# Adapter columns of each sample gathered on their own, in place of all adapters' columns, and weights of the next block loaded after three of four splits

## The reference, cut to what matters

```python
def _lora_linear(x, W, A, B, adapter_indices):
    base = jnp.einsum('bsd,df->bsf', x, W)
    Ai = A[adapter_indices]
    Bi = B[adapter_indices]
    lora = jnp.einsum('bsr,brf->bsf', jnp.einsum('bsd,bdr->bsr', x, Ai), Bi)
    return base + lora
gate = _lora_linear(x, Wg, Ag, Bg, adapter_indices)
up = _lora_linear(x, Wu, Au, Bu, adapter_indices)
h = jax.nn.silu(gate) * up
return _lora_linear(h, Wd, Ad, Bd, adapter_indices)
```

## Time and profile before

| | us |
|---|---|
| median of 3 runs | 1263.4 |
| lowest and highest | 1262.7, 1264.01 |
| profiled execution | 1261.51 |
| its span | 1259.5 |
| PE busy | 1248.5 |
| POOL busy | 665.2 |

### The profile page before, as it was taken

The page is one execution under the profiler, slowest core; times in us unless marked ns, Lnnn a source line. Parts: engine busy times, 40 slices in busy tenths (PEclk is TensorE's granted clock), DMA queues, the critical chain, the costliest instruction groups (busy, mean ns, idle before and its releaser), DMA issues.

```text
span 1259.5 us, 17908 instructions
## 1 busy us (share of the span) xinstructions
PE 1248.5 (99%) x6204; PEld 1042.1 (83%) x6204; DVE 976.8 (78%) x1554; ACT 559.4 (44%) x993; POOL 665.2 (53%) x549
## 2 busy tenths in 40 slices
PE   8999999999999999999999999999999999999998
PEld 7788888888888888888888888888888888888887
DVE  7987777886788777788779768777878877777775
ACT  4644445444344454454444444544443434434332
POOL 4476555555635556545554556565555444444553
PEclk9999999999999999999999999999999999999999
DMA  6856345555965345446687544544487732233423
GB/s 197 296 179 219 122 119 166 159 146 167 374 208 192 105 124 149 127 133 176 213 322 215 161 126 142 153 124 130 143 287 279 231 86 91 76 117 101 114 90 116
DMA packets 141096, 210.11 MB, mean 167 GB/s; under 512 B 43472, under 2 KB 87760, under 8 KB 141008
## 3 DMA queue, kind: packets, MB, share of 16 engines
q1 hardware_dynamic: 118128, 137.03, 35.2%
q0 software_dynamic: 22016, 70.80, 16.8%
q10 hardware_dynamic: 864, 1.15, 0.3%
HBM read 164.89 MB, written 44.04 MB: 166 GB/s over the span
## 4 chain that ended last, share of the span: by engine, by line
PE 91%; DVE 4%; DMA 2%; issue 1%; ACT 1%; another core or an unknown queue 0%; SPq 0%; DVEq 0%; ACTq 0%
PE px L1549 28%; PE pd L1549 27%; PE py L1549 14%; PE pz L1549 7%; PE pz L1566 3%; PE pv L1595 2%; PE pv L1593 2%; PE pd L1827 2%; PE py L1566 2%; PE px L1566 1%; DVE wg_lo L1215 1%; DMA w_raw<-w_gu 1%; PE pd L1576 1%; PE pd L1670 0%; PE pd L1798 0%
## 5 line engine op out<-in xcount | busy, mean ns | idle before, releaser
L687 POOL TENSOR_TENSOR h_lo<-g,h_hi 128x512 fp32r<-128x512 f32 x127 | 184.2, 1450 | 334.9 <-ACT h_hi L809 334.1
L656 POOL DMA_INDIRECT b_got<-b_table,idx_b x192 | 197.5, 1029 | 58.8 <-issue 49.3
L1549 PE MATMUL px<-xo_hi,wg_hi 128*128 128x512 f32 x540 | 216.8, 402 | 1.9 <-DVE xo_lo L1227 0.6
L1347 DVE TENSOR_TENSOR acc<-pd,acc 128x512 f32<-128x512 f32 x252 | 167.9, 685 | 63.2 <-PE pd L1549 57.6
L1215 DVE TENSOR_TENSOR wg_lo<-w_raw,wg_hi 128x512 fp32r<-128x512 f32 (+1 forms) x268 | 192.1, 720 | 31.5 <-ACT wg_hi L809 18.8
L1549 PE MATMUL px<-xo_hi,wg_lo 128*128 128x512 f32 x540 | 211.8, 392 | 0.0
L1549 PE MATMUL px<-xo_lo,wg_hi 128*128 128x512 f32 x540 | 210.3, 389 | 0.0
L809 ACT ACTIVATE wg_hi<-w_raw 128x512 fp32r<-128x512 f32 (+1 forms) x272 | 153.0, 570 | 115.1 <-PE py L1566 72.3
L1549 PE MATMUL pd<-wd_hi,h_hi 128*128 128x512 f32 x512 | 202.8, 396 | 0.0
L1549 PE MATMUL pd<-wd_lo,h_hi 128*128 128x512 f32 x512 | 201.0, 393 | 0.0
L1549 PE MATMUL pd<-wd_hi,h_lo 128*128 128x512 f32 x512 | 199.8, 390 | 0.0
(11 more groups left out here) (292 smaller groups left out, 2401.2 us busy)
## 6 DMA issues: line engine op xcount, KB each, us to landing
w_raw<-w_gu SPq DMA_DIRECT2D x68, 512.0 KB
wd_raw<-w_dn SPq DMA_DIRECT2D x64, 256.0 KB
xo_hi<-xops SPq DMA_DIRECT2D x21, 512.0 KB, 5.9
xo_lo<-xops SPq DMA_DIRECT2D x21, 512.0 KB, 6.9
acc<-x SPq DMA_DIRECT2D x8, 1024.0 KB, 8.3
ad_raw<-ad_table SPq DMA_DIRECT2D x16, 512.0 KB
xops<-st_hi SPq DMA_DIRECT2D x24, 256.0 KB, 2.8
xops<-st_lo SPq DMA_DIRECT2D x24, 256.0 KB, 2.9
```

The source lines that it names most:

```text
L656: gp.indirect_dma_start(out=dst, out_offset=None, in_=rows_of, in_offset=bass.IndirectOffsetOnAxis(ap=rows.bitcast(U32), axis=0)).then_inc ...
L687: return gp.tensor_tensor(dst, src_raw, src_hi, ALU.subtract)
L1347: ins = dve.tensor_tensor(dst, pd[j][:, :], dst, ALU.add)
L1549: ins = pe.matmul(psum, w_parts[wi], x_parts[xi], start=(start and i == 0), stop=(stop and i == 2), skip_group_check=more)
```

## The change

The columns of all eight adapters are no longer multiplied in quarters 2 to 4 (the first quarter is as it was, with its own code). Instead POOL gathers, for each of the quarter's 16 samples, the 32 input columns of its own adapter (`gather_own`: 16 gathers of 128 rows of 512 bytes) into `st_lo` in blocks 13 to 15. ACT and DVE split them in four groups, and PE multiplies them with the tokens in two pieces of 24 matmuls with 256 columns (`own_products`): one between the two last down phases, one after them. The 0/1 matrix no longer depends on the quarter: ACT makes it once, in block 14 of the first quarter, from masks that DVE makes in block 13. Small tables move into other buffers to make room. SP, POOL, ACT and DVE have a new order at the change of quarter, and `next_weights` waits for three groups and the sums, and skips the unit that has no weights any more. The diff, cut to its core; helpers and SP:

```diff
+        def own(cp):
+            return flat(st_lo[:, :, :]).rearrange("p (s c e) -> p s c e", s=QS, c=KC)[:, :, 2 * cp:2 * cp + 2, :]
...
+        def own_homes(g):
+            if g == 3:
+                return u[:, 0, 1, 0:2 * WH], u[:, 1, 1, 0:2 * WH]
+            return flat(wg_hi[:, 2 * g:2 * g + 2, :]), flat(wg_lo[:, 2 * g:2 * g + 2, :])
+        def summed_units(n):
+            return n - n // UNITS
...
             def next_weights(n):
-                for g in range(4):
+                if (n + 1) % UNITS == 0:
+                    return
+                for g in range(3):
                     sp.wait_ge(w_done[g], n + 2)
-                load_weights(n + 2)
+                sp.wait_ge(t_done, 4 * summed_units(n + 1))
+                load_weights(n + 2 if (n + 2) % UNITS else n + 3)
...
+                k_done = blocks_done(q, b)
+                if b == -1 and q:
+                    for g in range(2):
+                        store_ad(q, g)
+                if b >= 0 and b % AD_BLOCKS == 0 and n > 1:
+                    load_ad(q, b // AD_BLOCKS)
...
-                    for done, k in ((p1_mm, A11), (p5_mm, S1), (p6_mm, S2), (p2_mm, A12), (p7_mm, S3), (p3_mm, S4),
-                                    (p4_mm, A22)):
-                        sp.wait_ge(done, n)
+                    for done, k in ((p1_mm, A11), (p5_mm, S1), (p2_mm, A12), (p4_mm, A22), (p6_mm, S2), (p7_mm, S3),
+                                    (p3_mm, S4)):
+                        sp.wait_ge(done, k_done)
                         for g, xo in enumerate((xo_hi, xo_lo)):
                             sp.dma_start(raw(xo[:, k, :]), xops[g, k]).then_inc(xop_in[k], 16)
-                    next_weights(n)
...
+            def gather_own(q, samples):
+                for s in samples:
+                    home = flat(st_lo[:, :, :])[:, s * P:(s + 1) * P]
+                    gather_rows(home, a_in_rows, idx_own[:, (q - 1) * QS + s:(q - 1) * QS + s + 1], own_got[s // (2 * TP)])
...
+                if to_own and b % 2:
+                    if b == BLOCKS - 3:
+                        for half in range(2):
+                            gp.wait_ge(xops_out[half], TP * (q + 1) * 64)
+                    gather_own(q + 1, {-3: range(8, 11), -1: range(4, 7)}[b - BLOCKS])
...
                     gp.wait_ge(*piece_out(max(0, m - 1)))
-                    gp.wait_ge(p3_mm, n)
-                    gather_b(to_q, m, 0)
-                if b == BLOCKS - 2 and q + 1 < QUARTERS:
-                    for g in range(2, AD_GROUPS):
-                        gather_ad(q + 1, g)
+                    gp.wait_ge(p3_mm, k)
+                    if to_own and b == BLOCKS - 1:
+                        if q == 0:
+                            gp.wait_ge(bd_out, 2 * 16)
+                        else:
+                            gp.wait_ge(bdown_mm, q * QP)
+                        gp.wait_ge(xops_out[0], TP * (q + 1) * 64)
+                        gather_bd(q, 0)
+                    else:
+                        gather_b(to_q, m, 0)
...
-                    gp.wait_ge(p4_mm, n)
+                    gp.wait_ge(p4_mm, k)
+                    if to_own and b == BLOCKS - 1:
+                        gather_b(to_q, m, 0)
                     gather_b(to_q, m, 1)
...
-                    for half in range(2):
...
+                if to_own and b == BLOCKS - 1:
+                    for g in range(4):
+                        gp.wait_ge(w_done[g], n + 2)
                     for g in range(2):
                         gather_ad(q + 1, g)
-                if b == BLOCKS - 1 and q + 1 < QUARTERS:
```

ACT and DVE:

```diff
             def weights_high(n, g):
+                if n % UNITS == 0:
+                    if g < 3:
+                        act.wait_ge(own_got[g // 2], n // UNITS * 2 * TP * 16)
+                    else:
+                        act.wait_ge(own_diff, n // UNITS)
+                    src, hi_part, _ = own_group(g)
+                    copy(hi_part, src).then_inc(w_hi_done[g], 1)
+                    return
...
                 if b == -1:
...
                     v_lower(q - 1, 0)
                     v_high(q - 1, 0)
+                    ua_high(q, 0)
+                    weights_high(n + 1, 0)
+                    weights_high(n + 1, 1)
+                    weights_high(n + 1, 3)
                     v_lower(q - 1, 1)
...
+                    ua_high(q, 1)
+                    weights_high(n + 1, 2)
+                    v_high(q - 1, 1)
+                    continue
...
-                if b == -1:
-                    ua_high(q, 0, 0)
-                    ua_high(q, 1, 1)
-                    ua_high(q, 0, 1)
...
-                    v_high(q - 1, 1)
-                    weights_high(n + 1, 3)
-                    continue
+                if (q, b) == (0, BLOCKS - 2):
+                    act.wait_ge(sel_mm, 2)
+                    act.wait_ge(slots_done, 1)
+                    for m in range(2):
+                        for s in range(HS + 2):
+                            lo, hi = s * SAMPLE_ROWS, min((s + 1) * SAMPLE_ROWS, SEL_COLS)
+                            at = 2 * (s % HS) + m
+                            ins = act.activation(sel_own[:, m, :, lo:hi], pattern_kept[:, :, 0:hi - lo], ACT.Copy,
+                                                 scale=slot_mask[:, at:at + 1])
...
+                if to_own:
+                    for g in range(4):
+                        weights_high(n + 1, g)
...
+                dve.tensor_scalar(idx_own[:, :], adf[:, QS:SAMPLES], float(P), p_f[:, 7:8], ALU.mult, ALU.add)
...
+            def own_difference(q):
+                dve.wait_ge(own_got[1], q * 2 * TP * 16)
+                first, last_two = (own(cp)[:, 2 * TP:QS, :, :] for cp in range(2))
+                dve.tensor_tensor(last_two, last_two, first, ALU.subtract).then_inc(own_diff, 1)
...
                 if b == -1:
-                    v_low(q - 1, 0)
-                    c11(n)
-                    u3(n)
-                    ua_low(q, 0, 0)
-                    c12(n)
-                    ua_low(q, 1, 1)
-                    ua_low(q, 0, 1)
-                    sums(n + 1)
-                    weights_low(n + 1, 0)
-                    ua_low(q, 1, 0)
+                    ua_low(q, 1)
+                    finish(q - 1, 0, (0,))
+                    weights_low(n + 1, 2)
                     select(q, 0)
-                    weights_low(n + 1, 1)
-                    weights_low(n + 1, 2)
-                    finish(q - 1, 0)
-                    weights_low(n + 1, 3)
-                    selectors(q, 1)
+                    finish(q - 1, 0, (1, 2, 3))
                     continue
                 if b == 0:
                     if q:
                         v_low(q - 1, 1)
-                    c11(n)
-                    u3(n)
+                        sums(n + 1)
+                    c11(k)
+                    if q:
+                        weights_low(n + 1, 0)
+                    u3(k)
                     if not q:
                         sums(n + 1)
                     select(q, 1)
                     if not q:
...
-                        sums(n + 1, low=True)
...
+                if (q, b) == (0, BLOCKS - 3):
+                    dve.wait_ge(layer_mm, QP)
+                    dve.tensor_copy(pattern_kept, pattern)
+                    for at in range(2 * HS):
+                        ins = dve.tensor_scalar(slot_mask[:, at:at + 1], p_f[:, 0:1], float(at), None, ALU.is_equal)
+                    ins.then_inc(slots_done, 1)
+                if not last and not late and not to_own:
                     sums(n + 1)
                 if parts_at(q, b) is not None:
...
-                c11(n)
+                if to_own:
+                    own_difference(q + 1)
...
+                if to_own:
+                    sums(n + 2)
...
+                    if to_own and not phase_at[2]:
+                        v_low(q, 0)
+                        ua_low(q + 1, 0)
+                        weights_low(n + 1, 2)
+                        weights_low(n + 1, 3)
+                        for g in (0, 1, 3):
+                            weights_low(n + 2, g)
```

PE (removed: the branches `if adapters:` of the seven products):

```diff
             def select(q, t):
-                pe.wait_ge(ua_done, 4 * q + max(ua_order(q, t, m) for m in range(2)))
-                pe.wait_ge(sel_done, 2 * q + t + 1)
+                pe.wait_ge(ua_done, ua_made(q, t))
...
                         for part, ua in enumerate((h_hi, h_lo)):
-                            ins = pe.matmul(select_bank(q, t, m, c), sel[:, part, c * P:(c + 1) * P], ua[:, t, m, tokens],
-                                            start=(part == 0), stop=(part == 1))
+                            if q:
+                                first = c * P % SEL_REPEAT
+                                rows, ua_m = sel_own[:, m, part, first:first + P], ua[:, t, 0, tokens]
+                            else:
+                                rows, ua_m = sel[:, part, c * P:(c + 1) * P], ua[:, t, m, tokens]
```

(30 more changed lines are left out.)

313 lines of the change are left out of this document (159 added, 154 removed).

## The result

The changed kernel is slower: 1275.8 us median of four runs (1274.6 to 1278.1) against 1263.7 (1262.7 to 1264.65), a ratio of 1.0104 with a 95% interval of 1.0091 to 1.0117. The forecast was 1257.0, with a range up to 1262.8. The span went from 1259.5 to 1274.4 us.

What follows compares the result with a forecast made beforehand. PE bounds the kernel, busy 1248.5 of 1259.5 us. Per change 4.09 - 1.54 = 2.55 us; three give 7.65, less 1.2 paid once, 6.45 us: median 1263.4 becomes 1257.0, 8-in-10 range 1251.3 to 1262.8.

Steps and rivals of the forecast that it cites:

- The matmuls: PE at each change of quarter: 48 products at 0.1175 us, 5.64 us, replace 9.53 us of matmuls, gaining 3.89 us.
- the third rival: Weight loads not hidden in the 48 products: 188 ns each, 9.0 us per change, 1262.5 us; chance 0.03.
- Own columns in time: At `own_products`, from the end of block 15's first down phase: no PE wait, up to 0.3 us at the bound.
- Paid once: First quarter: selector copies in block 14 cost 1.0 us, index instructions 0.6, early loads return 0.4; sum 1.2 us.
- The new wait: Block 0 after each change: PE waits 1.54 us for masks that stand on DVE behind the load of block 1's weights.
- No gather landed later than 7.0 us, those in full stretches included: Argument against the rival of late own columns: every gather in the trace landed within 7.0 us.
- own columns that come late: Rival: PE waits at the first `own_products` for a split behind a late gather; slower, 1273.3 us; chance 0.05.
- Block 1: Block 1 of the new quarters: its wait for block 2's sums is covered, load out near 981.3, c11 due at 987.
- no queue at SP: Condition, with a quick gather, of the rival that block 1's weights land by 970.2: no new wait; chance 0.24.
- they land late: Rival: block 1's weights land at 974.2, wait 4.0 us, gain 0.05 us per change, 1264.5 us; chance 0.14.
- no new wait: Rival: block 1's weights land by 970.2, gain 4.09 us at each of three changes, 1252.3 us; chance 0.24.

Runs made afterwards that it cites:

- experiment 8: Kernel before, weights loaded after three groups and the sums instead of four groups: 1260.8 us, ratio 0.9990; experiment 3 with four groups again: 1256.5 us, ratio 0.9947.
- experiment 5: Kernel before, with only the changed kernel's order: next block's sums and splits ahead of c11 in blocks 0 and 1 of quarters 2 to 4; 1287.0 us, ratio 1.0190.
- experiment 7: Changed kernel without the loads of the tokens' low parts at each change of quarter (3.5 of 7 MB): 1261.8 us, ratio 0.9981.
- experiment 6: Changed kernel with 22 unused matmuls added on PE where it waits for the masks, block 0 of quarters 2 to 4: 1270.8 us, ratio 1.0066.
- experiment 1: Changed kernel with SP issuing the load of block 1's weights ahead of the two down-adapter stores: 1267.2 us, ratio 1.0043.
- experiment 2: Changed kernel with block 1's sums and splits back behind the gate in block 0 of quarters 2 to 4: 1266.0 us, ratio 1.0035.
- experiment 3: Changed kernel with the next block's sums and splits back behind the gate in blocks 0 and 1 of quarters 2 to 4: 1251.6 us, ratio 0.9912.
- experiment 4: Experiment 3 plus experiment 1's SP edit, block 1's weights loaded ahead of the stores: 1252.1 us, ratio 0.9913.

## Where the prediction held and where it failed

- **The matmuls** held: 48 products at 0.12 us, 5.74 us in place of 5.64. The weight loads were hidden and the third rival was wrong. The Trainium skill (TensorE: Matmul & The Clock Gate, The mechanism) says in its list of what overlaps that a load does so only in another row group, though the paragraph above that list also lets a load go ahead into a background weight buffer. The pitch of 0.12 us with a new weight for each product, where a load's row is 190 ns long, decides against the list here and fits the paragraph.
- **Own columns in time** held: PE waited neither at the first `own_products` nor at the second, in any of the three changes, and the 48 own gathers landed after 2.4 to 6.2 us.
- **Paid once**, forecast 1.2 us: the copies cost 0.87 us in block 14 (forecast 1.0), block 1 with the index instructions 0.16 (forecast 0.6), 0.5 us came back in blocks 2 to 12, as with the early loads in experiment 8, and the first mark was 0.43 us ahead already. The sum was 0.09. Of this the first mark is luck: between executions of code that is the same up to there it moves by over 1 us (1.4 us later in experiment 5 than in the kernel before).
- **The new wait** is the step that failed. Its mechanism was named rightly, place and releaser too, and the term of the sum was mis-sized: 1.54 us, where 6.19, 5.71 and 5.37 were measured. The working, against the start of block 0 at the third change (964.74 forecast, 974.86 measured): the second gather started 4.4 us ahead of it (3.2 forecast), but landed after 8.28 us and not some 5.2; so the weights' load was issued 4.4 us behind it (2.8 forecast) and let DVE start 10.8 us behind it (7.0 forecast). The two landings were the median of all such gathers and a load of block 14, from stretches with less under way (the share of the DMA engines is 0.67 from 919 to 927 us in the kernel before, and 0.98 from 970.5 to 978.8 us, while this gather is under way); for the traffic now beside them the prediction charged the time of one transfer, 1.3 us, and never added up the bytes. "No gather landed later than 7.0 us, those in full stretches included" was a misreading: the trace has a landing for 16 of the 296 gathers of that line, all of down adapters, the last one issued at 930.0 us, ahead of the token loads (938.05 us). The low parts of the tokens alone cost the gather 2.7 us (experiment 7). That "the token loads cannot hold the gather up for long" was argued, for the own gathers, from the Trainium skill (DMA: Bandwidth & Descriptors, Queues, rings and completion order): the own gathers bear it out, but engines may take turns between rings, and a gather of the down adapters still takes 8.28 us behind the token loads. The bound for "late" had the same fault, 4.0 us. A slower kernel had a chance of 0.07, and its case was another one, own columns that come late.
- **The clock** is missing from every case of the prediction. It was halved behind each of the three waits of over 5 us, which cost some 5 to 6.5 us in all (experiment 6): the waits cost their own 17.3 us and about a third more.
- **Block 1** failed, with a wait put at nothing: "c11 there is due only at 987". The change puts the sums of block 2 ahead of c11 in block 1 as well (`late`). c11 itself was in time; u3, which stands behind the sums, c11 and a split, was not, and PE waits 0.7 us for it. Block 1 gave away 1.93, 0.79 and 1.91 us; 0.9 us of each is this wait (experiment 6), and the other 1.0 us at the first and third change is the low clock of the first wait. In experiments 1 and 2, where block 0 has next to no wait, PE waits for c11 too, by up to 2.56 and 3.24 us.
- **The reason for the wait** was seen from one side. The prediction named the new place of the sums, but laid the length of the wait on POOL and SP, since the load stands behind the stores, and had no wait at all with "no queue at SP". Against block 0 the load is not later than it was: it went out at 974.67 in the kernel before (SP's timeline, below), 6.0 us behind the start of block 0, and now 4.4 us behind it. In the kernel before nothing in PE's path stood behind it: the first sum starts 11.9 us behind the start of block 0, with no wait (DVE's timeline), and in the changed kernel the load lets DVE start 11.6, 11.1 and 10.8 us behind it. It would have been in time for the old place.

```profile
974.67 0.33 SPq L483 DMA_DIRECT2D w_raw<-w_gu  x1
980.55 0.42 DVE L1202 TENSOR_TENSOR w_raw<-w_raw 128x256 f32<-128x256 f32 x1
```

  Experiments 3, 4 and 5 show it from both sides: with the old place of the sums the new SP order costs nothing, with the new place even the old SP order costs 24 us. Experiment 1 shows what the prediction had right: a load that goes out 0.3 us ahead of block 0 takes block 0's wait away too, but it is then some 4 us earlier than the changed kernel's and 6 us earlier than in the kernel before.

The rival "they land late" came closest, with no change as its end; the forecast of 1252.3 for "no new wait" is within 1 us of what the change gives without that order (1251.6), partly by luck: it gains less per change than was forecast (3.1 and not 4.09 us) and paid nothing once only, since the profiled execution was 0.9 us ahead at the end of the first quarter.

## What to carry to other kernels

An instruction that waits for a transfer makes everything behind it on its engine wait for that transfer: before moving it forward, compare when the transfer lands now, in the rows, with when the next thing behind it is due; here it was enough that the load had never been early enough for the new place, whatever its queue. Where a change packs transfers together, add up the bytes of the stretch and take landings from a stretch that is as full. And price a wait of some microseconds on TensorE at its length plus what a low clock behind it costs, here 1.4 to 2.5 us for a wait of 5.4 to 6.2 us.

## What was not expected of the hardware

- Behind 5.4 to 6.2 us without a matmul TensorE's granted clock was 0.50 and stayed there for 3.3 to 5.8 us of work; the products of 512 columns went from 0.23 to 0.43 us of pitch. With shorter waits it went either way: 2.56 us (experiment 1) and 2.33 us (experiment 2) were followed by a clock of 0.50, 2.25 us (experiment 1) and 2.57 us (experiment 7) were not. Executions of experiment 1 differ by 7 to 9 us, at mean clocks of 0.998 and 0.991 to 0.994.
- 66 matmuls of no use made the kernel about 5 us faster.
- A gather of 512 KB landed after 5.04 us with half of the token loads left out and after 7.3 to 8.3 us with all of them; the median of the earlier trace rows, 5.2 us, is from stretches with less traffic than these.
